# Two reorderings inside the steps of an attention pipeline: ScalarE's copies ahead of the exponential, TensorE's score product behind its other products

## The reference, cut to what matters

```python
qkv = x @ w_attn                                   # x after a layer norm
att = einsum('bhtd,bhsd->bhts', q, k) * scale + einsum('bhtd,tsd->bhts', q, rk)   # rk = embk[rel]
att = softmax(where(causal, att, -inf))
y = einsum('bhts,bhsd->bhtd', att, v) + einsum('bhts,tsd->bhtd', att, rv)         # rv = embv[rel]
x = x + y @ w_proj
# then x = x + experts(layernorm(x)): 2 shared and 8 gated hidden layers of 128
```

## Time and profile before

| What | us |
|---|---|
| median of three timed runs (862.37 to 868.55) | 867.35 |
| profiled execution, its own time | 863.58 |
| span of that execution, first to last instruction | 861.9 |
| first part, before the first exponential | 0 to 64.3 |
| attention slots, first exponential to the last | 64.3 to 625.4 |
| expert layer | about 630 to 861.9 |
| busy over the span: PE, DVE, ACT | 707.3, 598.7, 512.5 |

### The profile page before, as it was taken

How to read it: one execution, slowest core, us unless ns; L and a number is a source line. 1 busy time by engine, 2 the same in 40 slices (tenths; PEclk the granted TensorE clock), 3 DMA queues, 4 the chain that set the end, 5 groups by cost and what they waited for, 6 DMA issues and landing times. The chain is left out here.

```text
span 861.9 us, 27128 instructions
## 1 busy us (share of the span) xinstructions
PE 707.3 (82%) x10368; PEld 508.9 (59%) x10368; DVE 598.7 (69%) x2036; ACT 512.5 (59%) x1031; POOL 255.1 (30%) x253
## 2 busy tenths in 40 slices
PE   3657568878777887778887778887889999999998
PEld 2344356656555666566666656675666666666665
DVE  6835458777667786768886767777746777766776
ACT  2555567677677676768776767767652524544331
POOL 8333135523334443334552332553210000000000
PEclk9878779999999999999999999999999999999999
DMA  9789987577769666658867656775200000000000
GB/s 314 223 278 292 338 241 236 184 214 197 237 195 278 192 187 194 188 181 264 243 185 216 199 148 207 239 202 180 70 14 20 25 25 25 1 25 13 13 13 13
DMA packets 116687, 140.32 MB, mean 163 GB/s; under 512 B 8848, under 2 KB 83088, under 8 KB 116368
## 3 DMA queue, kind: packets, MB, share of 16 engines
q1 hardware_dynamic: 116560, 138.59, 53.3%
HBM read 82.26 MB, written 56.30 MB: 161 GB/s over the span
## 5 line engine op out<-in xcount | busy, mean ns | idle before, releaser
L906 ACT ACTIVATE work<-ps,nmin 128x128 f32<-128x128 f32 (+3 forms) x512 | 250.4, 537 | 146.6 <-DVE nmin L979 115.7
L979 DVE CUSTOM_DVE_ANT_0 ps<-ps,near 128x128 f32<-128x128 f32 (+3 forms) x512 | 242.1, 509 | 71.5 <-PE ps L759 38.9
L771 PE MATMUL ps<-ident,work 128*128 128x128 f32 x1280 | 216.0, 289 | 88.9 <-ACT work L895 83.6
L771 PEld LDWEIGHTS ps<-ident,work 128*128 128x128 f32 x1280 | 143.3, 145 | 129.8 <-ACT work L895 110.4
L964 DVE COPY work<-ps 128x512 f32<-128x512 f32 (+1 forms) x192 | 123.5, 643 | 77.2 <-PE ps L771 69.5
L720 POOL TENSOR_SCALAR_AFFINE_SELECT work<-work 128x512 f32<-128x512 f32 x96 | 60.9, 635 | 318.6 <-ACT work L895 303.4
L759 PE MATMUL ps<-kb,qb 128*128 128x128 bf16 (+3 forms) x512 | 131.9, 311 | 9.6 <-issue 8.3
L1298 ACT ACTIVATE near<-ps 128x512 f32<-128x512 f32 x80 | 47.6, 596 | 135.0 <-PE ps L1263 134.9
L724 POOL TENSOR_TENSOR work<-work 128x512 f32<-128x512 f32 x96 | 124.4, 1296 | 8.0
L1273 PEld LDWEIGHTS ps<-work,near 128*128 128x128 f32 x640 | 82.6, 191 | 34.3 <-issue 31.7
L788 PE MATMUL ps<-work,vb 128*9 128x128 f32 x2560 | 98.0, 282 | 5.2 <-ACT relS L884 4.7
(11 more groups left out here) (101 smaller groups left out, 642.7 us busy)
## 6 DMA issues: line engine op xcount, KB each, us to landing
near<-w_slots SPq DMA_DIRECT2D x96, 512.0 KB, 4.5
w_slots<-relS SPq DMA_DIRECT2D x128, 256.0 KB, 4.1
qk_rows<-work SPq DMA_DIRECT2D x48, 256.0 KB, 5.3
near<-w_slots SPq DMA_DIRECT2D x32, 256.0 KB, 4.6
w_slots<-near SPq DMA_DIRECT2D x8, 512.0 KB, 6.1
qb<-qk_rows SPq DMA_DIRECT2D x24, 96.0 KB
kb<-qk_rows SPq DMA_DIRECT2D x24, 96.0 KB
qb<-qk_rows SPq DMA_DIRECT2D x48, 48.0 KB
```

The costliest lines, as they stand in the source:

```text
L771: ins = nc.tensor.transpose(tp_ps[:, m % 2, n * P:(n + 1) * P], prob[:, m % PROBS, n * P:(n + 1) * P], ident[:, :])
L906: ins = nc.scalar.activation(prob[:, m % PROBS, h * wide:(h + 1) * wide], qk_ps[:, m % 3, h * wide:(h + 1) * wide], ACT.Exp, bias=nmin[:, ...
L979: nc.vector.tensor_tensor_reduce(out=scores, in0=scores, in1=near[:, q % NEAR, a, 4 * P - wide:4 * P, r], scale=1.0, scalar=3e38, op0=ALU. ...
```

## The change

TensorE issues the operations of `OPS[m]` before `qk(m + 1)` instead of after it. ScalarE copies turned unit m - 3 in slot m, where it copied m - 4, so the copy falls into the slot in which TensorE makes the turned unit; and it does that copy and the copies of `OPS[m]` before `exp(m)`. VectorE, GpSimd and SyncE keep their lists; no instruction is added or removed.

```diff
                 for m in range(SLOTS):
                     if 0 <= m - 3 < NU:
                         tp(m - 3)
+                    for kind, *what in OPS[m] if m else []:
+                        do[kind](*what)
                     if m + 1 < NU:
                         qk(m + 1)
                     if m == NU + 2:
                         pe.wait_ge(exp_done, NU)
                         experts["turn"](pe, 0)
-                    for kind, *what in OPS[m] if m else []:
-                        do[kind](*what)
...
                 for m in range(SLOTS):
-                    if 0 <= m - 4 < NU and on_act(m - 4):
-                        pT_copy(m - 4)
-                    if m < NU:
-                        exp(m)
+                    if 0 <= m - 3 < NU and on_act(m - 3):
+                        pT_copy(m - 3)
                     for kind, *what in OPS[m] if m else []:
                         if kind == "rel":
                             rel_copy(*what)
...
                         if kind == "yb":
                             turned_copy(*what)
+                    if m < NU:
+                        exp(m)
```

## The result

The changed kernel takes 853.69 us (median of four runs, 851.81 to 854.7) against 867.95 for the kernel before on the same chip: ratio 0.985, interval 0.980 to 0.989. That is 14 us faster. I had forecast 40, so the direction was right and the size was not. The two profiled executions, 863.58 before and 854.70 after, lie 8.9 us apart.

What follows compares the result with a forecast made beforehand. Engines waiting for each other were taken to bound rows 2 and 3, transfers mostly the first stage and row 0. Gains of 22.4 + 14.4 + 1.5 + 2.0 = 40.3 us gave 827 us, range 810 to 857.

Steps and rivals of the forecast that it cites:

- The copy behind an unrelated exponential: Rows 2 and 3: ScalarE's turned copy queues behind an exponential; transposes' 83.6 us idle behind it falls under 25.
- the four middle quads: Row 3 quads without tail operations: 1.2 us gained each, 0.2 in the four with tails; 22.4 us over four stages.
- VectorE's copy, whose slack I found near zero: Row 3: every second set of transposes waits for this copy; slack 0.2 us, so 0.25 us per quad stays lost.
- The slower rival: ScalarE held at a relative copy, TensorE then waiting for the exponential; row 1 loses 19 us, total 886; chance 0.08.
- the next limit of row 2: Relative tile's 8.8 us way through DRAM over 9.5 slots; six quads gain 0.8 us each, 14.4 us over three stages.
- The first stage: First stage of attention, bound mostly by the transfer of `near`: gain 1.5 us, between 0 and 5.
- Rows 0 and 1 together: All eight stages of rows 0 and 1: gain 2 us from earlier relative copies, between -4 and 8.
- The first rival: Rows 2 and 3: the wait mostly passes to VectorE's copy or late `near`; 17 us gained, 850 us; chance 0.20.

Runs made afterwards that it cites:

- moved puts: Changed kernel with puts of relative tiles issued from ScalarE's DMA queue behind the slot's exponential, instead of SyncE's: 830.69 us, ratio 0.955 to the kernel before.

## Why the prediction was wrong

**What held.** The copy behind an unrelated exponential did hold the transposes, and the wait went, but for the 9.6 us in small pieces. In row 3 I had costed the four middle quads at 1.2 us each. The middle 16 units fell from 23.6 to 19.2 and to 18.9 us in two groups, 1.1 and 1.2 a quad; transposes that before came at 317.18, 322.84 and 329.08 came 4.65 us apart, as two rows of the timeline after show:

```profile
312.55 0.65 PE L771 MATMUL ps<-ident,work 128*128 128x128 f32 x4
...
317.20 0.65 PE L771 MATMUL ps<-ident,work 128*128 128x128 f32 x4
```

VectorE's copy, whose slack I found near zero, did not become the wait: the page after lists 4.2 us of waits of that copy for transposes and none of transposes for it among the large ones. The slower rival, an exponential held behind a relative copy, wanted 19 us more in row 1, which went from 125.2 to 123.2 us. ScalarE's waits for relative products did grow, from 12.5 to 23.1 us; what they cost isn't shown.

**The step that failed** is the next limit of row 2: "So a slot can't go under 0.93 us, a quad under 3.7." I priced the way of one tile, 0.62 + 3.96 + 4.1, and divided it by the slots it has. That is a latency. The limit that I missed is a rate, and it lies in SyncE's list: get q, which waits for put q to land, stands ahead of put q+1. With both rows in hand, put at 359.19 and get at 363.15, I read a duration and not that the next put stood behind this get. That makes 4.0 to 4.6 us of landing and 0.6 of issue, 4.6 to 5.2 us a quad, where row 2 took about 5.0 before; there was almost nothing to win. I had written "SyncE's puts come earlier or at the same time, so its queue gains": the copies came earlier and the puts later. Freed of that list the changed kernel wins 4.8 to 5.9 us where I had said 4.8, in the first 24 units of the third and fourth groups (30.3 to 25.5, 32.8 to 26.9). The whole then comes to 831 us, and that this is near my 827 is in part luck: row 3 gave 14.8 us of 22.4 there, row 2 12.6 of 15.9 with its first stage, and rows 0 and 1 gave 6.3 where I had put 2.

The Trainium skill gives the fixed cost behind the 2.6 and 3.2 us that I set beside these rows (DMA: Bandwidth & Descriptors, "Anatomy of one DMA — SWDGE (gpsimd) path") for transfers that GpSimd issues. These are SyncE's, and the trace doesn't agree with it: the puts of row 2 in the third group took 3.9 to 4.6 us before and 4.4 to 5.0 after.

**Sizes.** Row 3 gave 13.0 us of 22.4. The middle units gave 12.2 of 19.2; some 4 us of the rest is the pause with the clock fall in the second group, which the second profile of the changed kernel did not have (19.8 us there). The same 16 units took 22.0 us with ScalarE's half alone, and 24.1, 18.8, 23.5 and 23.9 in four kernels with moved puts, so it comes and goes. The first 8 units lost 2.7 where I had counted on 1.6 of gain, the last 8 gave 3.5 instead of 1.6. The first stage gave 1.5 us, 54.2 to 52.7, as forecast, and that was luck: in the second profile it took 56.0. Rows 0 and 1 together gave nothing (185.6 before, 185.8 after), against 2 us. I had also written that rows 2 and 3 take 372 us; the stages add up to 375.

The first rival, 850 us, was nearest in time, and the transfer that it named besides VectorE's copy is what took over. Its sum was not right: it had 9.6 us from row 3 and 7.2 from row 2, and row 3 gave 13.0 and row 2 nothing. Two things stay open. The second group's row 2 took 33.9 us for its first 24 units even with moved puts. The expert weights and the next values are loaded there (from 219.80 in SyncE's list in the profile after, three transfers of 640 KB and one of 576), and with moved puts a put and a get issued at 214.19 and 215.31 took 9.5 and 10.7 us to land and VectorE waited 7.8 us for that get; no run moved the loads. And TensorE's half helps only together with ScalarE's; the waits above go with that, but no run tells which of them decides.

## What to carry to other kernels

When a wait is removed, ask of every queue that the shorter period needs how often it can go round, not only how long one item takes: write its list down in order and look for a wait that stands ahead of something ready. A queue that only issues transfers is an engine with a list like any other. And two limits of nearly the same size hide each other: here the one alone gave 0.3%, the other 1.5%, both 4.5%, so a small gain is a reason to look for the second limit, not to drop the first.

## What I had not expected of the hardware

In the third group's row 2 stage a put of 256 KB landed 3.9 to 4.6 us after its issue before the change, with the DMA engines 0.66 busy, and 4.4 to 5.0 us after it, with 0.67. Gets two slots later cost the kernel before 14 us, so these landings are close to the path even there. TensorE paused up to 3 us at its transposes and relative values with no releaser in the profile (19.9 and 16.6 us in all after the change, 4.8 and 11.3 before). Five of the six pauses over 2 us in the attention after the change go with a stretch at the 1.2 GHz level that begins within 2.3 us of the pause's end; the sixth, 2.96 us until 479.11, does not.

The packets in the trace say a little more about these pauses. The profiles before and after both have 84 transfers of 16 KB on the queue that the page calls instruction. Before the change all five pauses over 1.6 us in the attention ended 1.3 to 1.5 us after one of them had landed, and after it five of the six over 2 us ended 1.4 to 1.8 us after one. That speaks for TensorE waiting for instructions of its own, but no run tests it.
